# First cross attention of a two-layer gated block: fp32 products, resident weights, values for four heads at once

## What is computed

```python
def _L0_xattn_ref(x, latents, gamma_media, beta_media, gamma_lat, beta_lat, Wq, bq, Wkv, bkv, Wo, bo):
    xn = _layernorm(x, gamma_media, beta_media)        # the context
    ln = _layernorm(latents, gamma_lat, beta_lat)      # the tokens
    q = ln @ Wq + bq
    kv_input = jnp.concatenate([xn, ln], axis=1)
    k, v = jnp.split(kv_input @ Wkv + bkv, 2, axis=-1)
    q, k, v = (to_heads(q), to_heads(k), to_heads(v))  # 8 heads of 128
    q = q * DH ** (-0.5)
    attn = jax.nn.softmax(jnp.einsum('bhid,bhjd->bhij', q, k), axis=-1)
    out = jnp.einsum('bhij,bhjd->bhid', attn, v)
    return out.transpose(0, 2, 1, 3).reshape(b, -1, INNER) @ Wo + bo
...
x = x + jnp.tanh(g_xattn[0]) * _L0_xattn_ref(ctx_1024, _layernorm(x, axis=-1), ...)
```

## Time and profile before

| | |
|---|---|
| median of the runs | 3698.07 us (3697.74 to 3703.7, three runs) |
| profiled execution | 3702.21 us; its span, first to last instruction, 3700.5 us |
| first cross attention | 0 to 1783 us (first instruction of the next stage at 1783.1) |
| experts | 1783 to 2870 us |
| second cross attention | 2870 to 3340 us |
| feed-forward | 3340 us to the end |
| mean granted clock of PE | 0.951 of 2.4 GHz |
| busy over the span | PE 87%, PEld 77%, DVE 68%, ACT 47%, POOL 17% |

### The profile page before, as it was taken

One profiled execution on the slowest core, in us unless ns is written; L12 is line 12 of the kernel. 1 busy time (PEld: TensorE's weight loads), 2 busy tenths in 40 slices (PEclk: granted clock), 3 DMA queues, 4 the chain that ended last, 5 costly groups with the idle time before them and its releaser, 6 DMA issues. The chain is left out here.

```text
span 3700.5 us, 59440 instructions
## 1 busy us (share of the span) xinstructions
PE 3237.7 (87%) x19570; PEld 2862.3 (77%) x19570; DVE 2511.6 (68%) x4651; ACT 1736.3 (47%) x3190; POOL 617.7 (17%) x665
## 2 busy tenths in 40 slices
PE   4999899998999989999599999999999799993454
PEld 3999889998999989999466787878788688882333
DVE  5666766666666666666666767777776666668887
ACT  3555555555555555555333322232322466653454
POOL 3111111111111121110211111111110233320000
PEclk9999999999999999999799999999999799995677
DMA  3000000000000000000200100010000000000001
GB/s 83 7 11 13 6 13 12 13 6 13 13 6 13 12 12 7 11 1 1 49 0 0 23 0 23 0 23 0 1 0 0 19 1 0 0 0 23 0 0 46
DMA packets 79094, 43.13 MB, mean 12 GB/s; under 512 B 32031, under 2 KB 78168, under 8 KB 78936
## 3 DMA queue, kind: packets, MB, share of 16 engines
q1 hardware_dynamic: 78936, 41.12, 4.1%
HBM read 36.91 MB, written 4.19 MB: 11 GB/s over the span
## 5 line engine op out<-in xcount | busy, mean ns | idle before, releaser
L369 ACT ACTIVATE x_pth<-x_ps 128x512 fp32r<-128x512 f32 (+1 forms) x768 | 374.8, 526 | 265.3 <-PE x_ps L574 265.0
L462 DVE TENSOR_TENSOR x_ptl<-x_ps,x_pth 128x512 fp32r<-128x512 f32 (+1 forms) x768 | 435.6, 594 | 75.9 <-ACT x_pth L369 67.7
L374 ACT ACTIVATE x_p<-x_p,x_nmx 128x1178 f32<-128x1178 f32 x256 | 327.7, 1280 | 249.4 <-DVE x_p L479 249.4
L829 ACT ACTIVATE moe_sil<-moe_ps,moe_b 128x512 f32<-128x512 f32 x256 | 176.1, 688 | 553.2 <-PE moe_ps L988 544.9
L574 PE MATMUL x_ps<-ident,x_p 128*128 128x128 f32 x2560 | 371.2, 275 | 42.9 <-DVE x_ptl L462 42.9
L596 PE MATMUL x_ps<-x_pth,x_vh 128*128 128x256 f32 x1280 | 374.8, 293 | 1.6 <-DVE xres L498 1.6
L574 PEld LDWEIGHTS x_ps<-ident,x_p 128*128 128x128 f32 x2560 | 301.0, 141 | 93.1 <-DVE x_ptl L462 73.8
L596 PE MATMUL x_ps<-x_ptl,x_vh 128*128 128x256 f32 x1280 | 364.6, 285 | 0.0
L596 PE MATMUL x_ps<-x_pth,x_vl 128*128 128x256 f32 x1280 | 364.4, 285 | 0.0
L479 DVE TENSOR_SCALAR_CACHE_REDUCE x_p<-x_ps 128x1182 f32<-128x1182 f32 x256 | 354.4, 1384 | 9.6 <-PE x_ps L583 1.4
L939 DVE TENSOR_TENSOR moe_gf<-moe_sil,moe_ps 128x512 f32<-128x512 f32 x256 | 175.5, 686 | 174.2 <-ACT moe_sil L829 173.8
(11 more groups left out here) (361 smaller groups left out, 7908.0 us busy)
## 6 DMA issues: line engine op xcount, KB each, us to landing
x_wraw<-in_L_xattn_Wkv_dram SPq DMA_DIRECT2D x64, 128.0 KB, 2.3
xres<-in_x_dram SPq DMA_DIRECT2D x4, 1024.0 KB, 7.7
x_wraw<-in_L_xattn_Wq_dram SPq DMA_DIRECT2D x32, 128.0 KB, 2.3
x_wraw<-in_L_xattn_Wo_dram SPq DMA_DIRECT2D x32, 128.0 KB, 2.0
moe_w1r<-in_L_ffn_w_dram SPq DMA_DIRECT2D x8, 512.0 KB, 5.3
moe_w2r<-in_L_ffn_w_dram SPq DMA_DIRECT2D x4, 1024.0 KB, 8.7
out_dram<-xres SPq DMA_DIRECT2D x1, 4096.0 KB, 13.5
ffn_w<-in_L_ffn_w_dram SPq DMA_DIRECT2D x2, 1024.0 KB, 6.9
```

The lines of the kernel that those rows point to most:

```text
L369: act.activation(pth[:, (v // 2) % 2, lo:hi, (v % 2) * P:(v % 2 + 1) * P], ps[:, TURN + (v + g) % 2, 0:(hi - lo) * P].rearrange("p (n t) - ...
L374: act.activation(p[:, w % 4, DUP:DUP + R_KV], p[:, w % 4, DUP:DUP + R_KV], ACT.Exp, bias=nmx[:, w % 2:w % 2 + 1], scale=-1.0, accum_out=su ...
L462: dve.tensor_tensor(ptl[dst], ps[:, TURN + (v + g) % 2, 0:(hi - lo) * P].rearrange("p (n t) -> p n t", t=P), pth[dst].bitcast(F32), ALU.su ...
L829: act.activation(dst[:, q % 2, :], ps[:, HID + q % 2, :], ACT.Silu, bias=bias).then_inc(silu_done, 1)
```

## The change

`resample_stage` is written anew; nothing else of the program changes.

- Every product of the stage has fp32 operands: one product where three stood. The low parts and their tiles are gone, and so is all of POOL's work but two memsets.
- All weights of the stage stay in SBUF (`wk`, `wq`, `wv`, `wo`, 1 MB each, one DMA each, before the loops).
- Values are made for four heads at a time: a job takes 128 rows of the inputs as weights and streams 512 columns of `wv`, so the result is key by feature and isn't turned. Its bias is not added there: `bv @ wo` is computed once, added to `bo` and, times the gate, added to `xres` in steps 16 and 17 of each batch.
- Scores stand in 1178 adjacent columns of three banks, in pieces of 512, 512 and 154.
- A turned group is copied once: the first by ACT, the second and third by DVE. Values follow a step's turned blocks by two steps, the projection by one more, as before.
- The jobs of a batch are one list (`ORDER`): five of k and q a head, ten of v for heads 4 to 7 among those of heads 2 to 4, and during the last head the next batch's inputs, first k and q and first ten of v (`ENTRY`). `planned` spreads a head's jobs over its eight steps. The loops run over batches alone, 64 steps each.
- At the start the statistics are taken of the first batch's tiles and the context only; those of the other 24 tiles stand on DVE behind the first inputs.

```diff
-        LAG = 2
-        PLAN = [[0], [1], [2, 3], [4], [5], [6], [7, 8], [9, 10]]
+        TURN_LAG, PV_LAG, Y_LAG = 2, 4, 5
+        CUT = ((0, CH), (CH, 2 * CH), (2 * CH, R_KV))
+        MAKES = [kq(1), kq(2) + vals(1, 0, 4), kq(3) + vals(1, 4, 7), kq(4) + vals(1, 7, R_BLK), kq(5), kq(6), kq(7)]
+        ENTRY = [XJOBS[0:2], [], XJOBS[2:5], XJOBS[5:6] + kq(0)[0:2], kq(0)[2:5], vals(0, 0, 4), vals(0, 4, 7), vals(0, 7, R_BLK)]
+        def planned(b, w, after):
+            n, s = w // TPB, w % TPB
+            if n < R_HEADS - 1:
+                at, m = len(ENTRY_ALL) + sum(len(x) for x in MAKES[:n]), len(MAKES[n])
+                return [(b, at + i) for i in range(s * m // TPB, (s + 1) * m // TPB)]
+            at = sum(len(x) for x in ENTRY[:s])
+            return [(b + 1, at + i) for i in range(len(ENTRY[s]))] if after else []
...
+            sp.dma_start(wk[:, :, :], wkv[:, :, 0:R_INNER]).then_inc(d_w[0], 16)
+            sp.dma_start(wq[:, :, :], A["L0_xattn_Wq"].rearrange("(k p) n -> p k n", p=P)).then_inc(d_w[0], 16)
+            sp.dma_start(wv[:, :, :], wkv[:, :, R_INNER:2 * R_INNER]).then_inc(d_w[1], 16)
...
         @block.scalar
+                x = behind(w, TURN_LAG, 1, before)
+                if x is not None:
+                    act.wait_ge(turned, 3 * (STEPS * b + x) + 1 + TURN0)
+                    act.activation(turn_dst(x, 0), turn_src(x, 0), ACT.Copy).then_inc(a_kept, 1)
...
         @block.vector
+            def keep(b, x, g):
+                dve.wait_ge(turned, 3 * (STEPS * b + x) + g + 1 + TURN0)
+                dve.tensor_copy(turn_dst(x, g), turn_src(x, g)).then_inc(d_kept, 1)
+            def step(b, w, before, after):
+                if x is not None:
+                    keep(b, x, 1)
+                if w < STEPS:
+                    dve.wait_ge(s_done, W + 1)
+                    dve.wait_ge(turned, 3 * W - 9 + TURN0)
+                    dve.tensor_scalar(p[:, w % 4, 0:R_KV], scores[:, 0:R_KV], -1.0, R_BIG, ALU.mult, ALU.min,
+                                      accum_out=nmx[:, w % 2:w % 2 + 1]).then_inc(s_read, 1)
+                if x is not None:
+                    keep(b, x, 2)
...
         @block.tensor
-                        for w, x in ((wh, kvh), (wh, kvl), (wl, kvh)):
-                            last = pe.matmul(out[:, 0:hi - lo], w[:, n.j, i, k * P:(k + 1) * P], x[:, k, lo:hi],
-                                             start=(s == 0), stop=(s == 5))
+                        if kind == "v":
+                            last = pe.matmul(out, kvT[:, k, lo * P:(lo + 1) * P], wv[:, k, i * HALF * P:(i + 1) * HALF * P],
+                                             start=(k == 0), stop=(k == KT - 1))
+                        else:
+                            last = pe.matmul(out[:, 0:hi - lo], (wk if kind == "k" else wq)[:, k, i * P:(i + 1) * P], kvT[:, k, lo:hi],
+                                             start=(k == 0), stop=(k == KT - 1))
...
+            def turn(b, x, g):
+                if g < 2:
+                    pe.wait_ge(d_kept, 2 * X - 1 + g + D0)
+                else:
+                    pe.wait_ge(a_kept, X + 1)
...
-                for n in range(3):
-                    for i, (q, k) in enumerate(((qh, kh), (qh, kl), (ql, kh))):
-                        last = pe.matmul(scores[:, n, :], q[:, j, t * P:(t + 1) * P], k[:, j, SFROM[n]:SFROM[n] + SN],
-                                         start=(i == 0), stop=(i == 2))
+                for lo, hi in CUT:
+                    last = pe.matmul(scores[:, lo:hi], qT[:, n % 2, t * P:(t + 1) * P], kT[:, n % 2, lo:hi], start=True, stop=True)
...
-                    for i, (v, x) in enumerate(((vh, pth), (vh, ptl), (vl, pth))):
-                        last = pe.matmul(ps[:, PV, 0:2 * P], v[:, j, n * P:(n + 1) * P], x[:, u % 2, n, :],
-                                         start=(n == 0 and i == 0), stop=(n == R_BLK - 1 and i == 2))
+                    last = pe.matmul(ps[:, PV, 0:2 * P], v[:, n // HALF, c, (n % HALF) * P:(n % HALF + 1) * P], pT[:, u % 2, c, :],
+                                     start=(c == 0), stop=(c == R_BLK - 1))
...
+            for n in range(R_HEADS):
+                last = pe.matmul(ps[:, PV, 0:DIM], bvb[:, n, :], wo[:, n, :], start=(n == 0), stop=(n == R_HEADS - 1))
```

## The result

The changed kernel takes **3849.24 us** (median of 4 runs, 3845.17 to 3853.55) against 3697.9 beside it: ratio 1.0407, interval 1.0389 to 1.0425, slower. The forecast was 3835, in a range of 3800 to 3897.

The account below looks back on a forecast made before the run. TensorE was taken as the bound: first scores 63 + products 1806 + stalls 20 + issue 6 + rest 25 put the stage end at 1920, 137 us later; 3698 + 137 = 3835 us, range 3800 to 3897.

Parts of the forecast that it names:

- Bound and cover: First cross attention: TensorE, busy 1614 of 1714 us, sets the pace; VectorE's, ScalarE's and GpSimd's work is cover.
- The 95 us: TensorE's waits in the stage before: 46 us for values, 43 for low halves, 6 issue; the most shorter copies can return.
- The fp32 price: On TensorE: an fp32 product is two passes at 0.84 ns a column, 0.43 us against 0.36 for 256 columns.
- the rival of 0.19: Narrow score and k passes bound by their weight load, 0.19 us instead of 0.13: 38 us more, 3873; chance 0.10.
- The faster rival: 512-column fp32 passes cost 0.233 us, like an fp32r product: 354 us less, 3481; chance 0.03.
- Steps and jobs: TensorE's loop: 5.66 us a step without jobs, 1450 for 256 steps, plus 356 of jobs: 1806 us against 1574.
- Start: Before the loop: fewer statistics first, first turned input at 24 us, first scores at 63 against 69.
- Stalls: TensorE waits 0.47 us for VectorE at bare odd-to-even steps, about 1 us where inputs are kept: 20 us in all.
- The rest of 25 us: Allowance added to the stage's sum of 1895, from the 45 us left over before; stage end 1920.
- the 6 us of issue: TensorE's issue waits at the loops' edges, taken as 6 us as before.
- Clock in bare steps: Rival: the clock falls in some 36 bare steps, 1.7 us lost each, 61 us: 3896; chance 0.04.
- Another chain: Rival: a chain through VectorE and ScalarE paces the step, +60 us and more, 3895 or over; chance 0.04.

## Why the prediction was right

- **Bound and cover: right.** The copy that VectorE made twice cost nothing, and 52 us is all that 382 us less on VectorE brought the kernel before. **The 95 us as the most that shorter copies can return: not shown, and the reasoning failed.** With both large waits cut 87.5 us came back (3616.65 against 3704.18), but the whole list (the 95 and three small entries) fell only from 98 to 36 us by that: 1.4 us came back for each us of the list, in line with what single waits cost by the starts. Nor can its entries be taken one by one: 46 us removed alone returned nothing.
- **The fp32 price: right.** 0.43, 0.216 and 0.109 us as forecast. A narrow pass takes 0.14 by the weight loads above (1870.43 to 1870.57), so the rival of 0.19 fell. The Trainium skill (TensorE: Matmul & The Clock Gate, LDWEIGHTS) gives a load of 128 columns 107 ns. The distance of 0.14 leaves room for that; the records of the loads last 0.19, and no run here times a load by itself. The faster rival (0.233 for 512 columns) fell with the same rows.
- **Steps and jobs: right.** The pair of bare steps took 11.86 us, forecast 11.8 with its stall.
- **Start: 2 us off.** The first product stood at 25.5 (24 forecast), the first scores at 65.1 (63).
- **Stalls: too small.** The 36 waits at bare steps cost 22 us by the starts of the scores, not 17: 0.53 us each late in the last batch and 0.63 before it, for 0.47. I read the chain at the stage's end, where VectorE begins to read the scores 0.20 us after the last two blocks start. Inside the loop it begins 0.31 after them (295.52 and 295.83, above), and did so in the kernel before (1003.32 and 1003.64). At the crossings I had 1 us each, for inputs to be kept. There are waits of 2.84, 1.79 and 0.57 us and two stretches at a lower clock; 14.4 us of it came back when the latents were normalised earlier. I looked only for ScalarE's copies and not at what VectorE has to do ahead of the normalisation, whose place the diff showed.
- **The rest of 25 us** hid most of that, which is luck: it was half of an unexplained remainder of the kernel before. Stage end 1932.7 against 1920: 2 us from the start, 10.6 from the loop. Without the rest the loop would be 36 us short, and 42 without the 6 us of issue, which did not come. Of these, bare steps are 5, the waits at the crossings 13 (15.6 for 3) and the lower clock about 10; some 14 us stay open. The lower bound of the forecast itself was also summed wrongly: 3835 - 25 - 20 is 3790, not 3795.
- **Clock in bare steps:** 0.99 over the stage; the rival fell. Waits of 0.3 to 0.6 left it up. **Another chain:** fell.

## What to carry to other kernels

Price a change of number format by passes times columns, from start to start, before counting what it takes off engines that aren't the bound: here over 900 us of copies and splits left them, and a fifth more time per product, a seventh more of TensorE's work in the stage, decided. A list of the bounding engine's waits is no price for each: take what a wait costs from the starts of the instructions around it, here 0.63 for a listed 0.41. When one is removed, look at which chain is next and what stands ahead of it in its queues; a new table of jobs was worth nothing by itself, and 1.5% once the copies that TensorE waits for stood ahead of those it doesn't, with no work removed.

## What the runs showed of the hardware

- Three fp32r products cost less than one fp32 product at 256 columns (0.37, 3.66 us for thirty, against 0.432) and for the scores (2.58 against 2.86 us a step with the blocks before them), with operands of the same size: 152 us over this stage.
- A wait's length doesn't tell whether the clock falls. Behind the wait of 1.79 us at a crossing the scores took 3.61 us in the changed kernel and, with the latents normalised earlier, 2.15 at one crossing and 3.84 at another, though no other wait of more than 1 us stood near. Behind the wait of 2.83 or 2.84 us they took 2.89 in the changed kernel and 2.15 with the jobs on even steps.
- A wait of TensorE costs more than the profile's list of waits says: 0.53 for a listed 0.30, 0.63 for 0.41, and 0.52 for 0.20 in the kernel before.
